# The one-hot of the segment ends in the first layer: one broad VectorE comparison against four narrow ones

## The chip, the cores and the metric

The kernel runs on one core of one Trainium2 chip. The metric is the device time of a run in microseconds (us). The profile is of one execution of its own.

## The reference, cut to what matters

Two graph layers over 6250 nodes with 128 features and 206250 edges (200000 drawn ones, and a loop for each node), sorted by destination. The first layer takes, for each edge, two small matrix products with relu, and then for each destination the maximum over its edges:

```python
e = jnp.concatenate([h_i, h_j - h_i], axis=-1)
m = jax.nn.relu(e @ W2 + b2)
m = jax.nn.relu(m @ W3 + b3)
out = jax.ops.segment_max(m, dst, num_segments=N_NODES)
```

After it come a residual sum and a layer norm, then a second layer (softmax attention over the edges of a destination, a small perceptron, a norm over the nodes) and a last layer norm. The change touches the first layer alone.

## The kernel before

**Tiles and passes.** The edges are cut into 1612 tiles of 128. Four tiles make a group (`GT`), 13 groups a pass (`GROUPS`), and there are 31 passes, so the first layer has 403 groups. Each of the engines PE, ACT, DVE and SP runs a hardware loop over the passes with the 13 groups written out in it; the helper `groups` writes the stages of an engine in a fixed order, each stage some groups behind the newest one.

**GpSimd (POOL).** It writes out all 1612 gathers of the first layer one after the other (L453): each fetches the 128 rows of `q_tab` that a column of `srcT` names, and puts them into `G`. `G` holds a whole pass; a gather of group k waits only for the matmuls of group k - 13 that read its place. After the first layer POOL clears a buffer (L463, L464), and in the second layer it gathers rows of `x1_tab` by the same line.

**SyncE (SP)** loads a window of `p_tab` for each tile (L324) and two broadcast rows of `meta` for half a pass at a time (L332). The second kind waits until DVE has scanned the same half of the pass before.

**TensorE (PE)**, per group: `pre` (L740, L741: gathered rows and window summed in PSUM), `mm3` one group behind (L747), `tr_s` three behind (L753: the scanned maxima are transposed), and `pick` five behind (L762: the transposed maxima times the one-hot `EOH` of the segment ends, so that each segment's last running maximum lands in the column of its node).

**ScalarE (ACT)**, per group: two operations that make the one-hot `OH` (L534, L540), the relu (L545), and the copy out of PSUM after `tr_s` (L550).

**VectorE (DVE)**, per group, in this order: `add_up(0)` six groups behind (L977, adds a tile's picked columns to `accT`), `scan` two behind (L960, a running maximum over 512 edges), `add_up(1)`, `ends` four behind (L966), `add_up(2)`, `add_up(3)`. Each `add_up` waits for the one before it, since their columns may overlap, and reads where to add from a table of destinations (L239). `ends` is the operation that the change replaces: `endT[:, t]` holds for each edge of tile t the number of its node within the window if it is the last of its segment, and -1 otherwise; `EOH` is 1 where the number equals the column number. There are three `EOH` buffers in turn. PE waits in `pick` for the semaphore `eoh_ok`.

The names `Z`, `bank`, `iota_n`, `endT` in rows of the profile: `Z` is the large SBUF tensor that holds `OH`, `EOH`, `S` and other buffers, `bank` is PSUM, the others are SBUF tensors of their own.

Of the kernel before, what the change touches and what calls it, by code (L numbers as in the profile page):

```python
# [12 lines left out]
GT = 4  # L13
# [24 lines left out]
def build(nc, x, src, dst, W1, b1, W2, b2, W3, b3, we_dst, we_src, be, w_proj, b_proj,  # L38
          w1, bb1, w2, bb2, gamma, beta, out):
    fp32, bf16, i32 = mybir.dt.float32, mybir.dt.bfloat16, mybir.dt.int32  # L40
    ALU, ACT = mybir.AluOpType, mybir.ActivationFunctionType
    ds = bass.ds
# [15 lines left out]
    with ctx:  # L58
        def sb(name, shape, dt=fp32):
            return ctx.enter_context(nc.sbuf_tensor(name, shape, dt))  # L60

        def sem(name):
            return ctx.enter_context(nc.semaphore(name))


        ident, iota_n, ones = sb("ident", [128, 128]), sb("iota_n", [128, 128]), sb("ones", [128, 128])
        W1s, W2s, Wpq, W3s = sb("W1s", [128, 128]), sb("W2s", [128, 2, 128]), sb("Wpq", [128, 2, 128]), sb("W3s", [128, 128])
        wprojs, w1s, w2s = sb("wprojs", [128, 128]), sb("w1s", [128, 2, 128]), sb("w2s", [128, 128])
# [6 lines left out]
        srcT, relT, endT = sb("srcT", [128, TILES], i32), sb("relT", [128, TILES]), sb("endT", [128, TILES])  # L75
        rows = sb("rows", [128, TILES])
        cont = rows[0:1, :]
        base = rows[64:65, :].bitcast(i32)
# [13 lines left out]
        def z(shape, dt=fp32):  # L92

            n = 1
            for s in shape:
                n *= s
            words = n if dt != bf16 else n // 2
            assert top[0] + words <= ZW
            part = Z[:, top[0]:top[0] + words]
            top[0] += words  # L100
            assert top[0] <= ZW, top[0]
            if dt != fp32:
                part = part.bitcast(dt)
            if len(shape) == 2:
                part = part.rearrange("p (a b) -> p a b", a=shape[0])
            if len(shape) == 3:
                part = part.rearrange("p (a b c) -> p a b c", a=shape[0], b=shape[1])
            return part
# [19 lines left out]
        EOH = [z([GT, 128]) for _ in range(3)]  # L128
# [34 lines left out]
        consts, pads, prep = sem("consts"), sem("pads"), sem("prep")  # L163
# [7 lines left out]
        dist_ok, oh_ok, x_mm, relu_ok, v_mm, scan_ok, s_tr, st_ok, eoh_ok, o_mm, acc_ok = (sem(n) for n in (  # L171
            "dist_ok", "oh_ok", "x_mm", "relu_ok", "v_mm", "scan_ok", "s_tr", "st_ok", "eoh_ok", "o_mm", "acc_ok"))
# [18 lines left out]
        def after(eng, s, n):  # L191

            if not isinstance(n, int) or n > 0:
                eng.wait_ge(s, n)
# [42 lines left out]
        def bases(engine, t, n):  # L237

            _, got = nc.values_load_multi_w_load_instructions(base[0:1, ds(t, n)], engines=(engine,), min_val=0, max_val=NP - 128,  # L239
                                                             skip_runtime_bounds_check_because="a destination is a node, so below N")  # L240
            return got
# [17 lines left out]
        def used2(k, g):  # L259

            return k if g == 0 else k - 1

        def ring(g):
            return 2 if g == GROUPS - 1 else g % 2
# [147 lines left out]
        def _(pool):  # L412
# [4 lines left out]
            nc.gpsimd.memset(X[:, :, F + 1:TAB], 0.0).then_inc(pads, 1)  # L417
            nc.gpsimd.memset(X[:, :, F:F + 1], 1.0).then_inc(pads, 1)
            nc.gpsimd.iota(iota_n[:, :], pattern=[[1, 128]], base=0, channel_multiplier=0, allow_small_or_imprecise_dtypes=True).then_inc(consts, 1)
            nc.gpsimd.iota(neg_p, pattern=[[0, 1]], base=0, channel_multiplier=-1, allow_small_or_imprecise_dtypes=True).then_inc(consts, 1)  # L420
            nc.gpsimd.memset(ones[:, :], 1.0).then_inc(consts, 1)
            nc.gpsimd.memset(eps[:, :], EPS).then_inc(consts, 1)
# [4 lines left out]
                                    pattern=[[-1, 128]], channel_multiplier=1).then_inc(consts, 1)  # L427
# [27 lines left out]
            for k in range(PASSES * GROUPS):  # L455
                g = k % GROUPS
# [32 lines left out]
        def _(act):  # L489
# [11 lines left out]
                    act.dma_start(to, of.rearrange("(n a) -> n a", a=1)).then_inc(weights_in, 16)  # L501
                act.dma_start(BE, be.rearrange("(n a) -> n a", a=1).broadcast_to([128, 1])).then_inc(weights_in, 16)
            act.wait_ge(weights_in, 16 * 18)
            act.wait_ge(consts, 7)


            def x_evac(h, p, w):
# [180 lines left out]

        @block.tensor
        def _(pe):  # L690
            pe.wait_ge(consts, 7)

            def tr_x(h, p, w):
                pe.wait_ge(x_st[p], h - p + 2)
# [61 lines left out]
            def pick(k, g, i):  # L756

                pe.wait_ge(st_ok, k + 1)
                pe.wait_ge(eoh_ok, k + 1)
                after(pe, acc_ok, used2(k, g) * GT)  # L760
                for j in range(GT):
                    last = nc.tensor.matmul(bank[6 + g % 2][:, j * 128:(j + 1) * 128], STs[ring(g)][:, j * 128:(j + 1) * 128],  # L762
                                            EOH[ring(g)][:, j, :], start=True, stop=True)
                last.then_inc(o_mm, 1)

            groups(pe, [(0, pre), (1, mm3), (3, tr_s), (5, pick)])

            def tr_1(h, p, w):
# [127 lines left out]
        def _(dve):  # L896
            v = nc.vector
# [11 lines left out]
            v.tensor_copy(srcF[R], S0[R]).then_inc(prep, 1)  # L909

            dve.wait_ge(weights_in, 16 * 18)
            dve.wait_ge(consts, 7)
            v.tensor_copy(Wpq[:, 1, :], W2s[:, 1, :])

            v.tensor_tensor(wprojs[0:127, :], wprojs[0:127, :], wproj0[0:127, :], ALU.subtract)
# [47 lines left out]
            def ends(k, g, i):  # L963

                after(dve, o_mm, k - 1)
                v.tensor_tensor(EOH[ring(g)], iota_n[:, :].unsqueeze(1).broadcast_to([128, GT, 128]),  # L966
                                endT[:, ds(k * GT, GT)].unsqueeze(2).broadcast_to([128, GT, 128]), ALU.is_equal).then_inc(eoh_ok, 1)

            def add_up(j):
                def f(k, g, i):  # L970
# [7 lines left out]
                return f  # L978

            groups(dve, [(6, add_up(0)), (2, scan), (6, add_up(1)), (4, ends), (6, add_up(2)), (6, add_up(3))])  # L980


# [201 lines left out]
```

## Time and profile before

| | before |
|---|---|
| median of 3 runs | 4552.47 us (4547.58 to 4559.55) |
| profiled execution, its own time | 4550.18 us |
| its span, from the first to the last instruction | 4548.3 us |
| mean granted TensorE clock | 0.84 |
| POOL busy | 3277.4 us |
| first layer's gathers | 91.4 to 2151.2 us of the span |

Times in the rows are microseconds from the start of the span, or nanoseconds where "mean ns" or "duration ns" is said. A busy engine isn't the bound by that alone; what ended the idle time before an instruction tells more.

### The profile page before, as it was taken

What the parts mean: (1) busy time and instruction counts of PE and PEld (TensorE: products, weight loads), DVE (VectorE), ACT (ScalarE), POOL (GpSimd) and SP (SyncE); (2) the same over time, 40 slices, a digit from 0 to 9 for tenths busy, and PEclk for the clock granted to TensorE, in tenths of its full rate; (3) what the DMA queues carried; (4) which work ended last, traced back from release to release, by engine and by line L of the source; (5) the groups of instructions that cost most, each with busy time, mean ns of one, the idle gap of its engine ahead of it and who ended that gap; (6) DMA issues with size and microseconds to landing.
All of it is one profiled execution on the core that took longest, in us unless ns stands there. A gap on an engine that the chain in (4) does not pass through costs nothing.

```text
span 4548.3 us, 93656 instructions
## 1 busy us (share of the span) xinstructions
PE 3411.8 (75%) x19691; PEld 2455.3 (54%) x19691; DVE 2244.1 (49%) x5106; ACT 2123.6 (47%) x3882; POOL 3277.4 (72%) x3272
## 2 busy tenths in 40 slices
PE   4698888888888888888486666766777667676756
PEld 3587777777677777777244433433444344343432
DVE  2365555555555555555544444444444444444446
ACT  2454444444444444444445444544454454454434
POOL 3777777777777777777477777777777777777740
PEclk9899999999999999999657877787686777767767
DMA  5655555454555545454123223222222222232210
GB/s 124 182 172 164 152 154 158 144 168 144 165 151 152 159 145 166 146 165 116 62 75 81 75 74 79 77 74 74 78 77 75 75 81 75 75 81 74 75 42 28
DMA packets 409331, 503.91 MB, mean 111 GB/s; under 512 B 101159, under 2 KB 330081, under 8 KB 409118
## 3 DMA queue, kind: packets, MB, share of 16 engines
q1 hardware_dynamic: 301598, 284.83, 19.9%
q0 software_dynamic: 104832, 216.49, 19.3%
q14 instruction: 195, 1.60, 0.1%
q10 hardware_dynamic: 2690, 0.73, 0.1%
q8 instruction: 16, 0.26, 0.0%
HBM read 486.41 MB, written 15.26 MB: 110 GB/s over the span
## 4 chain that ended last, share of the span: by engine, by line
POOL 55%; issue 19%; PE 17%; DMA 4%; DVE 2%; SPq 1%; DVEq 1%; ACT 1%; POOLq 0%; ACTq 0%
POOL G L453 55%; PE bank L740 3%; PE bank L741 2%; PE bank L762 2%; PE bank L747 2%; DMA G<-q_tab,srcT 2%; PE bank L841 2%; PE bank L806 1%; PE bank L753 1%; DMA G<-x_tab,srcT 1%; SPq L282 1%; SPq L306 0%; PE bank L709 0%; PE bank L868 0%; DMA cont_d<-Z 0%
## 5 line engine op out<-in xcount | busy, mean ns | idle before, releaser
L453 POOL DMA_INDIRECT G<-x_tab,srcT x1612 | 1658.2, 1029 | 496.0 <-issue 486.5
L453 POOL DMA_INDIRECT G<-q_tab,srcT x1612 | 1568.7, 973 | 510.7 <-issue 484.7
L1091 DVE SCALAR_TENSOR_TENSOR Z<-Z,evr,bank 128x128 f32 x1612 | 560.7, 348 | 741.0 <-PE bank L841 605.3
L841 PE MATMUL bank<-Z 128*128 128x128 f32 x3224 | 860.6, 368 | 51.6 <-DVE Z L1091 50.1
L977 DVE TENSOR_TENSOR accT<-accT,bank 128x128 f32 x1612 | 452.3, 281 | 850.8 <-PE bank L762 620.4
L740 PE MATMUL bank<-ident,G 128*128 128x128 f32 x3224 | 669.3, 291 | 234.2 <-DMA G<-q_tab,srcT 185.6
L628 ACT ACTIVATE Z<-G,evr 128x128 f32<-128x128 f32 x1612 | 597.0, 396 | 424.9 <-PE bank L841 404.2
L841 PEld LDWEIGHTS bank<-Z 128*128 128x128 f32 x3224 | 564.5, 227 | 397.9 <-issue 253.1
L806 PE MATMUL bank<-Z 128*26 128x128 f32 x3224 | 715.8, 319 | 3.7 <-ACT Z L598 3.7
L740 PEld LDWEIGHTS bank<-ident,G 128*128 128x128 f32 x3224 | 519.6, 203 | 258.2 <-issue 257.5
L741 PE MATMUL bank<-Z 128*128 128x128 f32 x3224 | 655.1, 287 | 0.0
L960 DVE TENSOR_TENSOR_SCAN Z<-Z,bank 128x512 f32<-128x512 bf16 x403 | 515.7, 1280 | 79.1 <-PE bank L747 59.7
L741 PEld LDWEIGHTS bank<-Z 128*128 128x128 f32 x3224 | 520.8, 203 | 0.0
L747 PE MATMUL bank<-Z,W3s 128*128 128x512 f32 x806 | 432.5, 619 | 83.0 <-DVE Z L960 83.0
L545 ACT ACTIVATE Z<-bank 128x512 f32<-128x512 f32 x403 | 240.6, 597 | 543.1 <-PE bank L741 512.3
L550 ACT COPY Z<-bank 128x512 f32<-128x512 f32 x403 | 235.8, 585 | 505.2 <-PE bank L762 496.3
L762 PE MATMUL bank<-Z 128*128 128x128 f32 x3224 | 440.9, 281 | 11.7 <-DVE accT L977 11.7
L762 PEld LDWEIGHTS bank<-Z 128*128 128x128 f32 x3224 | 403.2, 197 | 19.6 <-DVE accT L977 15.5
L806 PEld LDWEIGHTS bank<-Z 128*26 128x26 f32 x3224 | 246.4, 114 | 215.8 <-issue 62.8
L753 PEld LDWEIGHTS bank<-ident,Z 128*128 128x128 f32 x1612 | 207.8, 145 | 223.0 <-issue 222.2
L534 ACT ACTIVATE Z<-Z,cols 128x512 bf16<-128x512 bf16 x403 | 291.6, 724 | 42.2 <-DMA Z<-meta 42.2
L813 PE MATMUL bank<-ident,G 128*26 128x128 f32 x124 | 37.7, 404 | 341.7 <-DMA G<-x_tab,srcT 341.7
(152 smaller groups left out, 2613.7 us busy)
## 6 DMA issues: line engine op xcount, KB each, us to landing
Z<-p_tab SPq DMA_DIRECT2D x1612, 64.0 KB
Z<-meta SPq DMA_DIRECT2D x62, 896.0 KB
Z<-meta SPq DMA_DIRECT2D x62, 832.0 KB
Z<-meta SPq DMA_DIRECT2D x62, 768.0 KB
G<-q_tab,srcT POOLq DMA_INDIRECT x1612
G<-x_tab,srcT POOLq DMA_INDIRECT x1612
Z<-ld_d SPq DMA_DIRECT2D x1612, 0.5 KB
x_tab<-X SPq DMA_DIRECT2D x13, 264.0 KB, 2.1
```

The lines of the kernel that those rows point to most:

```text
L453: return pool.indirect_dma_start(to, None, of, bass.IndirectOffsetOnAxis(ap=srcT[:, t:t + 1], axis=0))
L534: nc.scalar.activation(SQ[ring(g)], bc[:, 0, g * CH:(g + 1) * CH], ACT.Square, bias=neg_p).then_inc(dist_ok, 1)
L628: nc.scalar.activation(Gs[u], G[:, s * SC + j, 1:F + 1], ACT.Copy, scale=evr[:, s, 0, j:j + 1]).then_inc(gs_ok, 1)
L740: nc.tensor.matmul(o, G[:, g * GT + j, 0:F], ident[:, :], start=True, stop=False)
L741: last = nc.tensor.matmul(o, Pwin[:, g * GT + j, :], OH[ring(g)][:, j * 128:(j + 1) * 128], start=False, stop=True)
L747: nc.tensor.matmul(bank[2 + g % 2][:, :], W3s[:, :], M1[ring(g)], start=True, stop=True).then_inc(v_mm, 1)
L762: last = nc.tensor.matmul(bank[6 + g % 2][:, j * 128:(j + 1) * 128], STs[ring(g)][:, j * 128:(j + 1) * 128], EOH[ring(g)][:, j, :], start= ...
L806: nc.tensor.matmul(bank[4 + s][0:SC, 0:T], LWd[:, s, j * SC:(j + 1) * SC], OH2[j // HC][:, j % HC * T:(j % HC + 1) * T], start=(j == 0), s ...
L841: nc.tensor.matmul(bank[u][:, 0:128], Gs[u], EQ[j // HC][:, j % HC, :], start=True, stop=True).then_inc(t_mm, 1)
L960: v.tensor_tensor_scan(out=S[ring(g)], data0=bc[:, 1, g * CH:(g + 1) * CH], data1=bank[2 + g % 2][:, :], initial=NEG if first else S[ring( ...
L977: v.tensor_tensor(win, win, bank[6 + g % 2][:, j * 128:(j + 1) * 128], ALU.add).then_inc(acc_ok, 1)
L1091: v.scalar_tensor_tensor(out=win, in0=win, scalar=evr[:, s, 1, j:j + 1], in1=bank[(s * SC + j) % 4][:, 0:128], op0=ALU.mult, op1=ALU.add). ...
```

## The change

A second constant `iota_2` of 128 x 128 x 2 numbers holds every column number twice, and `iota_w` is every second element of it. `ends` becomes four VectorE instructions for a group, one for each tile: `iota_w` compared with one number per partition, column t of `endT`. Each of the four counts up `eoh_ok`, and `pick` waits for four times as many. POOL makes `iota_2` in its setup, so three engines wait for 8 constants in place of 7.

```diff
+        iota_2 = sb("iota_2", [128, 128, 2])
+        iota_w = iota_2[:, :, 0]
...
+            nc.gpsimd.iota(iota_2[:, :, :], pattern=[[1, 128], [0, 2]], base=0, channel_multiplier=0, allow_small_or_imprecise_dtypes=True).then_inc(consts, 1)
...
-            act.wait_ge(consts, 7)
+            act.wait_ge(consts, 8)
...
-                pe.wait_ge(eoh_ok, k + 1)
+                pe.wait_ge(eoh_ok, (k + 1) * GT)
...
                 after(dve, o_mm, k - 1)
-                v.tensor_tensor(EOH[ring(g)], iota_n[:, :].unsqueeze(1).broadcast_to([128, GT, 128]),
-                                endT[:, ds(k * GT, GT)].unsqueeze(2).broadcast_to([128, GT, 128]), ALU.is_equal).then_inc(eoh_ok, 1)
+                for j in range(GT):
+                    v.tensor_scalar(EOH[ring(g)][:, j, :], iota_w, endT[:, ds(k * GT + j, 1)], None, ALU.is_equal).then_inc(eoh_ok, 1)
```

## Rows read from the trace of the kernel before

**Rows 1.** The page: the chain that ended last, shares by engine.

```profile
POOL 55%; issue 19%; PE 17%; DMA 4%; DVE 2%; SPq 1%; DVEq 1%; ACT 1%; POOLq 0%; ACTq 0%
```

**Rows 2.** The page's groups of gathers: busy us, mean ns | idle before.

```profile
L453 POOL DMA_INDIRECT G<-x_tab,srcT x1612 | 1658.2, 1029 | 496.0 <-issue 486.5
L453 POOL DMA_INDIRECT G<-q_tab,srcT x1612 | 1568.7, 973 | 510.7 <-issue 484.7
```

**Rows 3.** All gathers of L453: ns min/median/max, and what ended POOL's idle time.

```profile
L453 POOL DMA_INDIRECT G<-q_tab,srcT x1612: 940/944/2559, 91.4 to 2150.2; - x180
...
  PE bank L741: 6.4, 21
```

**Rows 4.** Waits in the first layer (101 to 2150 us): us in total, times, longest.

```profile
PE bank L740 <- DMA G<-q_tab,srcT: 184.4, 97, 5.1
DVE accT L977 <- issue: 144.8, 40, 8.6
```

**Rows 5.** Timeline, a gather and an L966 that began before it: POOL, then DVE.

```profile
1184.12 1.17 POOL L453 DMA_INDIRECT G<-q_tab,srcT  x1 [0.30 <-issue]
...
1183.79 0.68 DVE L966 TENSOR_TENSOR Z<-iota_n,endT 128x512 f32<-128x512 f32 x1
```

**Rows 6.** Timeline, a gather and an L966 that began after it: POOL, then DVE.

```profile
1006.88 0.94 POOL L453 DMA_INDIRECT G<-q_tab,srcT  x1 [0.31 <-issue]
...
1007.15 0.68 DVE L966 TENSOR_TENSOR Z<-iota_n,endT 128x512 f32<-128x512 f32 x1
```

**Rows 7.** Timeline in the second layer, a gather begun under L1091: POOL, then DVE.

```profile
3104.49 0.94 POOL L453 DMA_INDIRECT G<-x_tab,srcT  x1 [0.31 <-issue]
...
3104.42 0.35 DVE L1091 SCALAR_TENSOR_TENSOR Z<-Z,evr,bank 128x128 f32 x1 [0.40 <-PE bank L841]
```

**Rows 8.** Timeline of the first three gathers of the first layer: DVE, then POOL.

```profile
91.49 1.02 DVE L934 TENSOR_SCALAR Z<-Z 124x1664 bf16<-124x1664 f32 x1
92.42 1.03 DVE L935 TENSOR_SCALAR Z<-Z 124x1664 bf16<-124x1664 f32 x1
...
93.79 1.89 DVE L940 TENSOR_TENSOR Z<-Z 124x1664 f32<-124x1664 int32 x1
95.71 1.03 DVE L941 TENSOR_SCALAR Z<-Z 124x1664 bf16<-124x1664 f32 x1
...
91.39 1.24 POOL L453 DMA_INDIRECT G<-q_tab,srcT  x1 [19.57 <-ACT relT L522]
92.94 1.34 POOL L453 DMA_INDIRECT G<-q_tab,srcT  x1 [0.30 <-issue]
94.58 2.28 POOL L453 DMA_INDIRECT G<-q_tab,srcT  x1 [0.30 <-issue]
```

**Rows 9.** VectorE groups by shape: busy us, mean ns | idle before.

```profile
L966 DVE TENSOR_TENSOR Z<-iota_n,endT 128x512 f32<-128x512 f32 x403 | 276.1, 685 | 0.0
...
L1003 DVE TENSOR_TENSOR mean<-stats 128x52 f32<-128x52 f32 x2 | 0.5, 250 | 0.1
...
L1005 DVE TENSOR_TENSOR tmp<-tmp 128x52 f32<-128x52 f32 x2 | 0.4, 213 | 0.1
...
L913 DVE COPY Wpq<-W2s 128x128 f32<-128x128 f32 x1 | 0.2, 219 | 0.0
...
L937 DVE TENSOR_SCALAR Z<-Z 124x13 f32<-124x13 f32 x1 | 0.2, 173 | 0.0
```

**Rows 10.** Timeline of DVE, one group's step and the start of the next.

```profile
1063.27 0.29 DVE L977 TENSOR_TENSOR accT<-accT,bank 128x128 f32 x1 [1.49 <-PE bank L762]
...
1064.96 0.68 DVE L966 TENSOR_TENSOR Z<-iota_n,endT 128x512 f32<-128x512 f32 x1
1065.56 0.28 DVE L977 TENSOR_TENSOR accT<-accT,bank 128x128 f32 x1
1066.00 0.29 DVE L977 TENSOR_TENSOR accT<-accT,bank 128x128 f32 x1 [0.15 <-DVE accT L977]
1067.25 0.29 DVE L977 TENSOR_TENSOR accT<-accT,bank 128x128 f32 x1 [0.96 <-PE bank L762]
```

More of the change, by code:

```diff
@@ L690, in _ @@
         def _(pe):
-            pe.wait_ge(consts, 7)
+            pe.wait_ge(consts, 8)
             def tr_x(h, p, w):
@@ L911, in _ @@
             dve.wait_ge(weights_in, 16 * 18)
-            dve.wait_ge(consts, 7)
+            dve.wait_ge(consts, 8)
             v.tensor_copy(Wpq[:, 1, :], W2s[:, 1, :])
```

## The prediction

> **What bounds the kernel now.** I read the chain that ended last first [rows 1]: 55% of the span is POOL and 19% is "issue"; PE, the busiest engine by the page, has 17% of the chain. POOL does almost nothing in that time but gathers [rows 2]: 1568.7 us of the first layer's 2060 are inside gathers, and 484.7 are the 0.30 us between two of them that nothing but issue explains. The reader is to see that POOL never rests for anybody: its waits for PE come to 6.4 us in the whole layer [rows 3]. PE, on the contrary, waited 184.4 us for gathered rows [rows 4], some 6 us in each of 31 passes. So the first layer is as long as 1612 gathers with their gaps, and the work of DVE, where the change is made, costs only what it does to the gathers.
>
> Next the spread of one gather [rows 3]: minimum 940, median 944, but mean 973 ns [rows 2]. A few are much longer. The excess is 1612 x (973 - 944) = 46.7 us. The first four gathers take 1.24, 1.34, 2.28 [rows 8] and 2.56 us (the maximum in [rows 3], the fourth in order), which is 3.6 us over four times 0.944, beside setup work that stays as it is. 43.1 us are left. Which instruction do they come from? The timeline shows it. The gather that starts at 1184.12 takes 1.17 us; an L966 had begun at 1183.79 and ended at 1184.47, 0.35 us into the gather [rows 5]. Where an L966 starts after the gather did, the gather takes its 0.94 us [rows 6]. So a gather does something near its start (it reads its column of `srcT`) that can't be done while L966 runs, and it goes on when L966 ends; the extra time is what is left of L966 less 0.12 us (0.35 - 0.12 = 0.23 = 1.17 - 0.94). L966 is the one VectorE operation of this layer that reads two SBUF tensors; L977 and L960 read one and a bank of PSUM. As a check: gathers start every 1.28 us, and a block of h us placed by chance costs (h - 0.12)²/(2 x 1.28) us. For h = 0.685 [rows 9] that is 0.125 us, times 403 is 50 us, near the 43 that are there. The Trainium skill, SBUF — State Buffer, section Who interferes with whom, says the same: a VectorE instruction with two SBUF inputs contends with a GpSimd instruction that reads SBUF. The trace agrees, by the 43 us.
>
> **The change, part by part.**
>
> 1. *L966 goes.* With it goes its hold on the gathers: -43 us, if what replaces it holds nothing. Its own 0.685 us of DVE time don't lie on the path.
>
> 2. *Four comparisons come, one SBUF row and one number per partition each.* What do they hold? Two bounds. The lower one is nothing: L1091 reads an SBUF tensor, a bank and a number per partition out of SBUF, and a gather that starts 0.07 us after it takes 0.94 us [rows 7]. That has the number per partition, and one SBUF tensor, as the new instruction has. The upper bound is in setup [rows 8]: L934, L935 and L941, comparisons with one SBUF tensor, run at two elements a cycle (1664 elements in 1.03 us, against 1.89 for L940 on as many), and they do hold gathers, at two places. The second gather begins at 92.94 under L935 (until 93.45) and is 0.40 us too long, 0.51 - 0.12: the place near its start. And the first ends at 92.63, 0.12 after L934; the third at 96.86, 0.12 after L941: a second place some 0.82 us into a gather, which L966 doesn't touch. So it matters whether the new instruction runs at the double rate. All those that do, and are long enough to be told, read their row in steps of one. The new one reads in steps of two. The one comparison with a stepped source is L937, 13 elements in 173 ns [rows 9]; from the 0.15 to 0.16 us that any operation takes beside its elements, one a cycle gives 0.17 to 0.18 and two a cycle 0.165 to 0.175. It doesn't decide. I take the single rate, hold nothing, -43 us, and price the double rate below.
>
> 3. *How long are they?* At the single rate 128 elements take 0.26 to 0.29 [rows 10]; the number per partition adds up to 0.07 (L1091's 0.35 [rows 7] against L977's 0.28); the steps add up to 128 x (250 - 213)/52 ns = 0.09, from L1003 with stepped sources against L1005 without [rows 9]. So 0.28 to 0.44 each. Two successive operations overlap by about 0.08 (L966 would end at 1065.64, L977 begins at 1065.56 [rows 10]), so four take 0.9 to 1.5 in place of 0.68: +0.2 to +0.8 us a group.
>
> 4. *What hides it.* DVE's step lasts 3.02 us from 1063.27 to 1066.29, then 0.96 idle for PE [rows 10]; the loading of the next destinations, which I estimate at 0.5 of that idle time, comes on top. 3.5 + 0.8 = 4.3 us against 4 x (0.944 + 0.30) = 4.98 that POOL needs for a group. Over a pass of 13 groups 8.8 us are left, and DVE's loop turn takes about 144.8/40 = 3.6 us of issue [rows 4]. DVE fits. It is late by up to 0.8 us for `scan` and `add_up` of the next group, and so is PE where it follows DVE; PE's 184 us of waiting for rows cover that. If the cover were gone, 0.8 x 403 = 322 us would show. SP's broadcast waits for scans; a scan that is 1 us late moves it by 1 us of the pass that it has.
>
> 5. *Small ones.* The larger constant: POOL writes 256 elements more ahead of its list loads, which I put at +0.3 (one element a cycle or two, as VectorE's rows have it). Three more semaphore counts: nothing waits for the first three alone. The register work for three more columns of `endT` is done while the scan before it runs. At the layer's end the last comparisons follow one another with nothing to hide them: +1.
>
> Sum: 4550.2 - 43.1 + 0.3 + 1 = 4508.4 for an execution like the profiled one. The median of the runs is 2.3 us above it, so 4511 us, 0.9% faster. The second layer has 1612 x (1029 - 944) = 137 us of the same delays [rows 2], from another line; where its comparisons fall against the gathers will shift by chance, which I estimate at 10 us either way.
>
> **The rivals.**
>
> *Both ports, at little or even cost.* If the stepped comparison runs at the double rate it holds gathers at both places. With a hold of h, four in each group, the delay is 1612 x (h² + (h - 0.12)²)/(2 x 1.25) us. For h: L913, a copy of 128 elements at the double rate, takes 0.219 [rows 9]; less the overlap 0.14; with the number per partition 0.21; with the steps 0.25. That gives 13, 34 and 51 us, against the 43 that go: 30 faster, 9 faster, 8 slower. So about 4520 at the low end and 4540 to 4560 in the middle, no change that can be told. For it: part 2's own rows; against it: steps of one in all of them. The Trainium skill speaks for this rival: Vector Engine (DVE) Microarchitecture Reference, section Performance modes — why throughput varies by op and dtype, names for the two-port mode one source, both tensors in SBUF and an even outermost extent, and no condition on the step. No row here shows it.
>
> *Both ports, dear.* If successive ones don't overlap, h is 0.33 and the delay 98 us: 55 slower, 4607. If a waiting gather weren't let in between two of the four, they would act as one block of 1.0 us: 403 x (1.0² + 0.88²)/2.5 = 286, 243 slower, 4795. Against the last: the third gather got its first place between L940 and L941, 0.03 us apart [rows 8]. It decides from h = 0.23.
>
> *DVE becomes the bound.* At 0.6 us a comparison its step is 3.5 + 1.5 = 5.0 us, a pass 65 + 3.6 = 68.6 against 66.4 now (13 x 4 x 1.278): 31 x 2.2 = 70 slower, 4620. It decides from about 0.5 us each; the rows give at most 0.44.
>
> *It does nothing:* the gathers are held by something else that comes in the same moment, and stay at 973 ns. 4552. Against it: the sum from L966 alone, 50 us, leaves nothing of the 43 for another cause.
>
> **How the numbers follow.** Forecast (hold nothing) 0.45. Both ports: little cost 0.10, even 0.25, dear 0.11. DVE bound 0.04. Nothing happens 0.05. A measurement of this kernel tells 0.3%, 14 us, from no change. Faster: 0.45 and 0.10, less 0.01 for chance in the second layer, 0.54; same 0.30; slower 0.16. The likeliest case alone spans 4500 to 4523. The range for 8 in 10 reaches over the even case and part of the dear one: 4497 to 4580.
>
> **What the profile after would show.** Right: first layer's gathers with mean near 946 ns, the last of them starting near 2108 in place of 2150, POOL's waits for PE still under 20 us, the new line 1612 times at 0.28 to 0.44 us. Both ports: the new line at 0.22 to 0.33 us, with many gathers of 1.0 to 1.25 us. DVE bound: POOL waits for PE, and PE no longer for rows. The prediction is wrong if the stepped read doesn't keep the instruction to one port.

## The result, and the profile after

The changed kernel takes 4523.35 us (median of 4 runs, 4518.22 to 4528.1) against 4551.94 for the kernel before in the same session (4 runs, 4547.58 to 4559.55). The ratio is 0.9935, with a 95% interval of 0.9921 to 0.995: 28.6 us, 0.65% faster. The profiled execution of the changed kernel took 4528.10 us, the longest of its four; its span is 4526.3 us, its granted clock 0.837.

The page of the changed kernel: the chain's shares, then groups with busy us, mean ns | idle before. L456 is what L453 was, L970 the new comparison, L980 the old L977, L744 the old L741.

```profile
POOL 53%; issue 20%; PE 16%; DVE 4%; DMA 4%; DVEq 2%; SPq 1%; ACT 1%; POOLq 0%; ACTq 0%
...
L456 POOL DMA_INDIRECT G<-x_tab,srcT x1612 | 1664.6, 1033 | 495.9 <-issue 486.4
L456 POOL DMA_INDIRECT G<-q_tab,srcT x1612 | 1531.2, 950 | 509.9 <-issue 483.2
...
L970 DVE TENSOR_SCALAR Z<-iota,endT 128x128 f32<-128x128 f32 x1612 | 361.6, 303 | 0.0
```

The gaps are what they were (483.2 against 484.7 in [rows 2]); the first layer's gathers lost 37.5 us. The instructions of L456 in the changed kernel (ns min/median/max, first and last start in us, and what ended POOL's idle time):

```profile
L456 POOL DMA_INDIRECT G<-q_tab,srcT x1612: 940/944/2558, 93.2 to 2114.5; - x180
L456 POOL DMA_INDIRECT G<-x_tab,srcT x1612: 940/944/2732, 2208.3 to 4362.9; - x180
...
  PE bank L744: 7.9, 26
```

The median gather is the same and POOL still waits for nobody; the excess over the median shrank from 44.7 us to 7.2 (counting the 1608 gathers behind the first four), and the last gather starts at 2114.5 where it started at 2150.2 [rows 3].

The waits of the changed kernel between 101 and 2150 us (us in total, times, longest):

```profile
PE bank L750 <- DVE Z L963: 127.4, 30, 5.4
PE bank L743 <- DMA G<-q_tab,srcT: 103.7, 47, 5.1
```

PE waits 103.7 us for rows in place of 184.4 [rows 4]: faster gathers use up its cover and don't exhaust it.

The two profiled executions, added up in us (before, after, difference):

| | before | after | |
|---|---|---|---|
| first gather starts | 91.4 | 93.2 | +1.8 |
| gathers of the first layer, busy | 1568.7 | 1531.2 | -37.5 |
| last `q_tab` gather starts | 2150.2 | 2114.5 | -35.7 |
| second layer's gathers, busy | 1658.2 | 1664.6 | +6.4 |
| span | 4548.3 | 4526.3 | -22.0 |

Between -35.7 and -22.0 lie some 0.8 us at the first layer's end and 12.7 us in the second layer, whose code is the same: 6.4 of them are gathers, the rest is at its end. The runs of the changed kernel spread over 10 us, and the profiled one is the slowest of them; the medians differ by 28.6. In the +1.8 there is POOL's new constant (POOL's setup: busy us, mean ns):

```profile
L422 POOL IOTA iota<- 128x256 f32 x1 | 1.5, 1513 | 0.0
...
L421 POOL IOTA iota_n<- 128x128 f32 x1 | 0.2, 235 | 0.0
```

It moves the issue of the list load `in_src` from 10.58 to 12.07 us. But the list itself comes 5.4 us later (timeline of VectorE, before, then after):

```profile
33.03 1.03 DVE L909 CAST Z<-Z 124x1664 f32<-124x1664 int32 x1 [32.91 <-DMA Z<-in_src]
...
38.46 1.03 DVE L912 CAST Z<-Z 124x1664 f32<-124x1664 int32 x1 [38.34 <-DMA Z<-in_src]
```

And in the experiments below the first gather starts anywhere from 92.5 to 96.4 us with this same setup, at 92.3 in the kernel before. So how much of the 1.8 is the constant isn't shown.

**Where ports are met.** Four comparisons in the changed kernel, undisturbed (timeline: start us, us):

```profile
1001.75 0.87 DVE L970 TENSOR_SCALAR Z<-iota,endT 128x128 f32<-128x128 f32 x4
```

Each takes 0.28 and the next starts 0.196 after it. Here a gather starts under them:

```profile
1108.51 1.04 POOL L456 DMA_INDIRECT G<-q_tab,srcT  x1 [0.30 <-issue]
...
1108.06 0.87 DVE L970 TENSOR_SCALAR Z<-iota,endT 128x128 f32<-128x128 f32 x4
```

The third of the four runs at 1108.51, from 1108.45 to 1108.73. The gather is 0.10 us too long: 0.22 less 0.12, the rule of [rows 5], for the one comparison that runs and not for the block that lasts until 1108.93. So the gather is let in between two of the four. In all, 131 gathers are more than 10 ns above the median, by 6.3 us together, and none by more than 0.11. That is less than the 0.16 that a comparison of 0.28 us could give, because a comparison that has only just begun doesn't delay a gather: of the 35 gathers that start 0.02 to 0.06 us after a comparison does, 33 keep their 0.94 us. And here the comparisons meet the middle of a gather:

```profile
760.74 0.94 POOL L456 DMA_INDIRECT G<-q_tab,srcT  x1 [0.31 <-issue]
...
761.21 1.02 DVE L970 TENSOR_SCALAR Z<-iota,endT 128x128 f32<-128x128 f32 x4
```

The gather has its 0.94, and the block takes 1.02 in place of 0.87: one of the four was held. The line's durations show how often and how much (its mean is 303, the page says):

```profile
L970 DVE TENSOR_SCALAR Z<-iota,endT x1612: 259/282/515, 164.6 to 2132.8; 128x128 f32<-128x128 f32 x180
```

Those that are held begin 0.48 to 0.75 us into a gather. That is DVE's time, and DVE has time here.

### The profile page after: what moved, and what is told of

It is laid out like the page before. It is cut to its first block, busy times and chain, and to the rows that moved or that the text cites. A ratio compares the mean times of both kernels' runs of the same rounds, so it can differ in the third digit from the quotient of the medians.

```text
span 4526.3 us, 96396 instructions
## 1 busy us (share of the span) xinstructions
PE 3399.4 (75%) x19691; PEld 2442.7 (54%) x19691; DVE 2322.8 (51%) x6315; ACT 2123.9 (47%) x3882; POOL 3247.6 (72%) x3273
## 4 chain that ended last, share of the span: by engine, by line
POOL 53%; issue 20%; PE 16%; DVE 4%; DMA 4%; DVEq 2%; SPq 1%; ACT 1%; POOLq 0%; ACTq 0%
POOL G L456 53%; PE bank L844 2%; PE bank L765 2%; PE bank L743 2%; PE bank L750 2%; PE bank L744 2%; PE bank L809 2%; DMA G<-q_tab,srcT 1%; PE bank L756 1%; DVE accT L980 1%; DVE Z L970 1%; DMA G<-x_tab,srcT 1%; DMA Z<-in_src 1%; SPq L308 0%; PE bank L712 0%
## 5 line engine op out<-in xcount | busy, mean ns | idle before, releaser
L456 POOL DMA_INDIRECT G<-x_tab,srcT x1612 | 1664.6, 1033 | 495.9 <-issue 486.4
L456 POOL DMA_INDIRECT G<-q_tab,srcT x1612 | 1531.2, 950 | 509.9 <-issue 483.2
L1094 DVE SCALAR_TENSOR_TENSOR Z<-Z,evr,bank 128x128 f32 x1612 | 560.8, 348 | 740.9 <-PE bank L844 599.8
L980 DVE TENSOR_TENSOR accT<-accT,bank 128x128 f32 x1612 | 452.2, 281 | 684.5 <-PE bank L765 478.5
L743 PE MATMUL bank<-ident,G 128*128 128x128 f32 x3224 | 648.6, 284 | 148.8 <-DMA G<-q_tab,srcT 103.7
L744 PE MATMUL bank<-Z 128*128 128x128 f32 x3224 | 640.8, 281 | 0.0
L743 PEld LDWEIGHTS bank<-ident,G 128*128 128x128 f32 x3224 | 507.0, 198 | 161.8 <-issue 161.1
L750 PE MATMUL bank<-Z,W3s 128*128 128x512 f32 x806 | 447.7, 639 | 127.4 <-DVE Z L963 127.4
L744 PEld LDWEIGHTS bank<-Z 128*128 128x128 f32 x3224 | 507.0, 198 | 0.0
L970 DVE TENSOR_SCALAR Z<-iota,endT 128x128 f32<-128x128 f32 x1612 | 361.6, 303 | 0.0
```

The lines of the kernel that those rows point to most:

```text
L456: return pool.indirect_dma_start(to, None, of, bass.IndirectOffsetOnAxis(ap=srcT[:, t:t + 1], axis=0))
L743: nc.tensor.matmul(o, G[:, g * GT + j, 0:F], ident[:, :], start=True, stop=False)
L744: last = nc.tensor.matmul(o, Pwin[:, g * GT + j, :], OH[ring(g)][:, j * 128:(j + 1) * 128], start=False, stop=True)
L750: nc.tensor.matmul(bank[2 + g % 2][:, :], W3s[:, :], M1[ring(g)], start=True, stop=True).then_inc(v_mm, 1)
L970: v.tensor_scalar(EOH[ring(g)][:, j, :], iota_w, endT[:, ds(k * GT + j, 1)], None, ALU.is_equal).then_inc(eoh_ok, 1)
L980: v.tensor_tensor(win, win, bank[6 + g % 2][:, j * 128:(j + 1) * 128], ALU.add).then_inc(acc_ok, 1)
```

## The experiments

**What chips they ran on.** The chips that took the experiments run this kernel in about 5900 us, before the change or after it, and every comparison below is with runs of the kernel before on the same chip. The groups of the kernel before there (busy us, mean ns | idle before):

```profile
L453 POOL DMA_INDIRECT G<-x_tab,srcT x1612 | 1605.9, 996 | 1433.3 <-ACT Z L628 973.8
...
L453 POOL DMA_INDIRECT G<-q_tab,srcT x1612 | 1527.7, 948 | 959.8 <-remote 476.8
```

The median gather lasts as long as elsewhere (946 ns), but POOL stands still between them. Its timeline, PE, then ACT, then POOL:

```profile
1048.39 0.39 PE L741 MATMUL bank<-Z 128*128 128x128 f32 x2
...
1051.58 0.60 ACT L545 ACTIVATE Z<-bank 128x512 f32<-128x512 f32 x1 [3.88 <-remote]
...
1049.31 0.95 POOL L453 DMA_INDIRECT G<-q_tab,srcT  x1 [0.30 <-issue]
1051.74 0.95 POOL L453 DMA_INDIRECT G<-q_tab,srcT  x1 [1.48 <-remote]
```

L545 waits for matmuls that end near 1048.8, and begins 2.8 us later. The same place in the changed kernel on its first chip:

```profile
1012.68 0.39 PE L744 MATMUL bank<-Z 128*128 128x128 f32 x2
...
1013.20 0.60 ACT L548 ACTIVATE Z<-bank 128x512 f32<-128x512 f32 x1 [0.67 <-PE bank L744]
```

It begins 0.1 us after the matmuls' end. Over all groups the median of this delay is 2.7 us in the one case and 0.12 in the kernel before on its first chip. PE's word to the others comes late on the experiments' chips, a group takes 6.1 us in place of 5.0 (the mean from scan to scan), and gathers don't bound the first layer. Nor the second one: POOL waits 973.8 us there for ACT's L628, where it waited 4.6 on the first chip, and TensorE's granted clock is 0.52 in that layer (nearly all of it at the lower level, 1.2 GHz) where it was 0.76; in the first layer it is 0.92 against 0.94. So **the total time can't decide there what the change is worth where gathers bind**; what can be read is the length of each gather and of each comparison. The table has both. "Delayed" counts, of 1608 gathers (all but the first four), those more than 10 ns above the run's own median, and "by" is the sum of what they are above it; on the first chip these were 179 and 43.9 us before the change, 131 and 6.3 after it. "First layer" is from the fifth gather's start to the last one's, in the profiled execution.

| run | comparison, for a group | ratio [95%] | gather mean ns | delayed | by, us | median ns of one | first layer, us |
|---|---|---|---|---|---|---|---|
| before_again | one, two tensors, 512 | (one run, 5919.29) | 948 | 8 | 0.6 | 684 | 2458.4 |
| e0_after_again | four, step 2 | 1.0022 [1.0013, 1.0031] | 948 | 22 | 0.8 | 281 | 2469.9 |
| e1_step1 | four, step 1 | 1.0025 [1.0013, 1.0036] | 948 | 12 | 0.4 | 281 | 2462.4 |
| e8_step1 | the same | 1.0028 [1.0017, 1.0039] | 946 | 14 | 0.6 | 281 | 2466.4 |
| e2_narrow_tt | four, two tensors | 1.0024 [1.0013, 1.0035] | 952 | 63 | 6.9 | 285 | 2464.0 |
| e6_narrow_tt | the same | 1.0035 [1.0022, 1.0047] | 952 | 61 | 6.6 | 284 | 2466.9 |
| e9_halves_tt | two, two tensors, 256 | 1.0002 [0.9993, 1.0012] | 953 | 267 | 9.1 | 418 | 2462.4 |
| e4_broad_ts | one, step 2, 512 | (one run, 5908.39) | 953 | 88 | 7.6 | 537 | 2451.4 |
| e3_no_ends | none | 0.9885 [0.9869, 0.9902] | 948 | 1 | 0.1 | - | 2447.9 |
| e7_no_ends | none | 0.9884 [0.9868, 0.9901] | 945 | 2 | 0.1 | - | 2452.7 |
| e5_second_layer | as after, and the second layer's split | 1.0333 [1.0316, 1.035] | 948 | 18 | 0.7 | 281 | 2466.8 |
| e10_second_again | the same | 1.0385 [1.0369, 1.0401] | 946 | 15 | 0.5 | 281 | 2469.8 |

Means that differ by 2 or 3 ns say nothing of delays here: the median itself is 944 to 947 ns from run to run.

**The two kernels again**, with no edit in either.

> The changed kernel once more, on the chip of the following runs. In the runs so far the kernel before takes 5900 us, not 4552, and there PE's semaphore after L744 is raised 2.9 us after that matmul begins (0.29 us in the first profile), so the steps of PE, ACT and DVE last over 6 us and not the gathers bound the first layer. If that holds here too: the freed gathers gain nothing, and the longer DVE step costs 0.2 to 0.9 us in a part of the groups, ratio 1.001 to 1.005. If the kernel before takes 4552 here: ratio 0.992 to 0.995.

> The kernel before with a profile on this chip, as the counterpart of the runs here. Where steps and not gathers bound the first layer: L966 holds gathers as before (single delays up to 0.5 us), but POOL waits for PE in every group, so that the delays vanish in those waits. In the first layer DVE's idle time for PE is longer than 1.2 us in a step.

The 43 us of delays are not there even in the kernel before: 0.6 us are. With the group's rhythm fixed by PE, its L966 misses the gathers' starts. The change costs 13 us there (0.2%).

**The row in steps of one.** All else as in the change:

```diff
-                    v.tensor_scalar(EOH[ring(g)][:, j, :], iota_w, endT[:, ds(k * GT + j, 1)], None, ALU.is_equal).then_inc(eoh_ok, 1)
+                    v.tensor_scalar(EOH[ring(g)][:, j, :], iota_n[:, :], endT[:, ds(k * GT + j, 1)], None, ALU.is_equal).then_inc(eoh_ok, 1)
```

> The four comparisons of the changed kernel, but they read the constant row in steps of one. The changed kernel's comparison takes 282 ns, and up to 515 where it begins 0.48 to 0.75 us into a gather. Theory H (it runs at the double rate and holds both ports whatever the step; what helped is that each of the four is short): 0.22 to 0.28 us each at the median, still up to some 0.5 us in the same place of a gather, gathers of the first layer 948 to 951 ns in the mean, time within 5 us of the changed kernel's 4523 us. Theory S (the step of two keeps the comparison to one port, and that is why the gathers are freed): the step-one comparison holds gathers at two places, their mean goes to 955 to 970 ns, 10 to 30 us slower than the changed kernel.

> The same kernel as e1_step1 (the four comparisons read the constant row in steps of one), once more, in order to have its time where the gathers bound the first layer. If the step does nothing: ratio 0.992 to 0.995, as the changed kernel's 0.9935. If the step of two were what helps: 0.996 to 1.002.

The comparison, first with steps of one and then, on such a chip too, the changed kernel's with steps of two:

```profile
L970 DVE TENSOR_SCALAR Z<-iota_n,endT x1612: 260/281/503, 188.0 to 2626.9; 128x128 f32<-128x128 f32 x180
```

```profile
L970 DVE TENSOR_SCALAR Z<-iota,endT x1612: 259/281/519, 192.1 to 2636.8; 128x128 f32<-128x128 f32 x180
```

The two agree in minimum and median, in the maximum to 16 ns, and the ratios agree: the step does nothing. So both hold one port pair or both hold two; the broad form tells which.

**One broad comparison of the new kind**, with 512 elements. It compares all four tiles with the first one's numbers, so the other three tiles' ends are left out.

```diff
-                for j in range(GT):
-                    v.tensor_scalar(EOH[ring(g)][:, j, :], iota_w, endT[:, ds(k * GT + j, 1)], None, ALU.is_equal).then_inc(eoh_ok, 1)
+                v.tensor_scalar(EOH[ring(g)], iota_w.unsqueeze(1).broadcast_to([128, GT, 128]), endT[:, ds(k * GT, 1)], None, ALU.is_equal).then_inc(eoh_ok, GT)
```

> One comparison of 512 elements with one number per partition (all four tiles are compared with the first tile's ends, so three of four are wrong), the row in steps of two. It tells rate and hold. Double rate: 0.42 to 0.67 us. Single rate: 0.75 to 1.1 us. If it holds both ports (theory H), gathers are held by what is left of it at their start, 403 x (h - 0.12)^2/2.5 us, 15 us for 0.42 and 49 for 0.67, and perhaps at their second place too: mean 955 to 980 ns. If one SBUF row in steps of two holds nothing, the mean is 946 ns whatever the length.

```profile
L969 DVE TENSOR_SCALAR Z<-iota,endT x403: 461/537/710, 192.6 to 2617.5; 128x512 f32<-128x512 f32 x135
```

Undisturbed it takes 0.48 us. At one element a cycle 512 take L966's 0.685 [rows 9] and the number per partition comes on top; so it runs at the double rate. Two meetings with gathers in its timeline, POOL and DVE:

```profile
1360.28 1.20 POOL L456 DMA_INDIRECT G<-q_tab,srcT  x1 [0.30 <-issue]
...
1360.19 0.48 DVE L969 TENSOR_SCALAR Z<-iota,endT 128x512 f32<-128x512 f32 x1
...
220.74 1.00 POOL L456 DMA_INDIRECT G<-q_tab,srcT  x1 [0.30 <-issue]
...
221.15 0.48 DVE L969 TENSOR_SCALAR Z<-iota,endT 128x512 f32<-128x512 f32 x1
```

The first is the place near the start: 1360.67 - 1360.28 - 0.12 = 0.27, and the gather is 0.26 too long. The second begins 0.41 us into a gather and ends at 221.63; the gather ends at 221.74, 0.11 after it and not at 221.69. That is the second place of [rows 8], reached by the stepped comparison when it is long enough. Up to 710 ns of its own are the third meeting: it began later in a gather and was held itself, as more than half of these comparisons are (the median is 537 ns, not 480).

**Four narrow ones with two tensors**, the old kind in the new size:

```diff
-                    v.tensor_scalar(EOH[ring(g)][:, j, :], iota_w, endT[:, ds(k * GT + j, 1)], None, ALU.is_equal).then_inc(eoh_ok, 1)
+                    v.tensor_tensor(EOH[ring(g)][:, j, :], iota_n[:, :], endT[:, ds(k * GT + j, 1)].broadcast_to([128, 128]), ALU.is_equal).then_inc(eoh_ok, 1)
```

> Four operations for a group as in the changed kernel, but each is the old kind: tensor_tensor of the constant row and the tile's column of end numbers, both read from SBUF. Theory H (length of one hold counts: what is left of the operation at the gather's start, less 0.12 us): operations of 0.28 us some 0.2 apart hold gathers no more than the changed kernel's, the mean is 948 to 952 ns, and the time is within 5 us of 4523 us. Since this kind isn't held by a gather's writes, it stays at 0.28 us with no tail to 0.5. Theory O (one SBUF row in place of two is what freed the gathers): two SBUF rows hold as before, mean 965 to 975 ns, time 4545 to 4555 us.

> The same kernel as e2_narrow_tt, four tensor_tensor operations with two SBUF rows, once more, in order to have its time where the gathers bound the first layer. Theory H (length of a hold): within 5 us of the changed kernel, about 0.993 of the kernel before. Theory O (one SBUF row in place of two): 1.000 of it.

```profile
L970 DVE TENSOR_TENSOR Z<-iota_n,endT x1612: 266/285/341, 189.6 to 2630.0; 128x128 f32<-128x128 f32 x180
...
762.75 1.09 POOL L456 DMA_INDIRECT G<-q_tab,srcT  x1 [0.30 <-issue]
...
762.13 0.89 DVE L970 TENSOR_TENSOR Z<-iota_n,endT 128x128 f32<-128x128 f32 x4
```

(One row of the line's durations, two of the timeline.) It is as long as the new kind, 285 against 281 ns, and it delays gathers near their start by the same rule (0.27 - 0.12 = 0.15). But its longest is 341 ns where the new kind's is 515: in the middle of a gather it isn't held. That is one thing that tells the two kinds apart. The other is how soon they hold. The gather above starts 0.02 us after the last of the four comparisons and waits for it all the same. A gather of e1_step1 that starts as soon after the last of its four (at 360.69) doesn't wait:

```profile
360.73 0.95 POOL L456 DMA_INDIRECT G<-q_tab,srcT  x1 [0.30 <-issue]
...
360.11 0.88 DVE L970 TENSOR_SCALAR Z<-iota_n,endT 128x128 f32<-128x128 f32 x4
```

Of the gathers that start 0.02 to 0.06 us into a comparison, 25 of 25 are delayed in e2 and 21 of 22 in e6; of the new kind's, none of 107 in e0, 1 of 111 in e1 and none of 58 in e8. So in a like rhythm the old kind delays gathers by 6.9 and 6.6 us, the new kind by 0.4 to 0.8. The time doesn't part them: e1 and e2 are equal, e6 is within e8's interval.

**Two halves with two tensors.**

```diff
-                for j in range(GT):
-                    v.tensor_scalar(EOH[ring(g)][:, j, :], iota_w, endT[:, ds(k * GT + j, 1)], None, ALU.is_equal).then_inc(eoh_ok, 1)
+                for j in range(0, GT, 2):
+                    v.tensor_tensor(EOH[ring(g)][:, j:j + 2, :], iota_n[:, :].unsqueeze(1).broadcast_to([128, 2, 128]),
+                                    endT[:, ds(k * GT + j, 2)].unsqueeze(2).broadcast_to([128, 2, 128]), ALU.is_equal).then_inc(eoh_ok, 2)
```

> Two operations of the old kind for a group, 256 elements each, two SBUF inputs. Between one of 512 (43 us of held gathers) and four of 128 (7 to 10). Length of a hold: (0.42 - 0.12)^2/2.5 us for each, 806 of them, 29 us, if they fall on the gathers by chance; in a fixed rhythm with them anything from 10 to 40. Longest single delay (a gather's length less 0.944): about 0.42 - 0.12 = 0.3 us, against 0.51 under the long operation and 0.15 under the short. By number of SBUF inputs alone all three would be alike.

```profile
883.46 1.20 POOL L456 DMA_INDIRECT G<-q_tab,srcT  x1 [0.30 <-issue]
...
883.42 0.75 DVE L970 TENSOR_TENSOR Z<-iota_n,endT 128x256 f32<-128x256 f32 x2
```

The first half runs from 883.42 to 883.84, 0.38 us beyond the gather's start, and the gather is 0.26 too long. Had the pair held as one block, until 884.17, it would have been 0.59. Its ratio is no change, the least of the split forms' cost.

**No comparison at all.** The one-hot is filled once ahead of the layer, and DVE's comparison in each group is left out, so that the maxima are picked at wrong columns:

```diff
-            groups(dve, [(6, add_up(0)), (2, scan), (6, add_up(1)), (4, ends), (6, add_up(2)), (6, add_up(3))])
+            groups(dve, [(6, add_up(0)), (2, scan), (6, add_up(1)), (6, add_up(2)), (6, add_up(3))])
...
-                pe.wait_ge(eoh_ok, (k + 1) * GT)
+                pe.wait_ge(eoh_ok, 9)
```

> No comparison in the loop: the three buffers are filled once ahead of the first layer with the ends of the first tiles and never again, so the maxima are picked at wrong columns. It is the floor: what is left of the delays, and what the four comparisons cost DVE. If the 6 us of delays that are left in the changed kernel come of the comparisons: mean 946 ns (the first four gathers alone), layer's gathers 6 us shorter than the changed kernel's, 4512 to 4520 us. If another operation holds gathers too, the mean stays at 949 to 950.

> The same kernel as e3_no_ends (no comparison in the loop, the picked maxima are wrong), once more, in order to have its time where the gathers bound the first layer. The whole of what the comparisons cost: first layer's gathers at 946 ns, 43 us less than the kernel before in the gathers, ratio 0.990 to 0.992. A ratio below 0.985 would say that DVE's own time lies on the path too.

Both are 1.15% faster, 68 to 70 us, and that isn't the price of the comparisons. The gathers of e7, and of the kernel before on such a chip (first and last start):

```profile
L456 POOL DMA_INDIRECT G<-q_tab,srcT x1612: 938/944/2558, 92.6 to 2553.9; - x180
L456 POOL DMA_INDIRECT G<-x_tab,srcT x1612: 938/944/2186, 2688.8 to 5651.0; - x180
```

```profile
L453 POOL DMA_INDIRECT G<-q_tab,srcT x1612: 939/946/2556, 92.3 to 2559.3; - x180
L453 POOL DMA_INDIRECT G<-x_tab,srcT x1612: 939/946/2396, 2698.5 to 5731.8; - x180
```

The first layer's gathers end 5 us earlier, the second layer's take 2962 us from first to last in place of 3033, in code that is the same. They are shorter themselves, 974 to 977 ns in the mean where every run with a comparison and the same second layer has 996 or 997, which is some 35 of the 71 us. Why the second layer went faster wasn't tried. In the first layer the old comparison costs 6 to 11 us on these chips (2458.4 less 2452.7 and 2447.9), and no more can be taken from these runs.

**The second layer's comparisons split in the same way.** The second layer's broad comparison, 1664 elements of two tensors, becomes 13 narrow ones:

```diff
-                v.tensor_tensor(EQ[c], iota_n[:, :].unsqueeze(1).broadcast_to([128, HC, 128]),
-                                relT[:, ds(q * SC + c * HC, HC)].unsqueeze(2).broadcast_to([128, HC, 128]), ALU.is_equal).then_inc(eq_ok, 1)
+                for j in range(HC):
+                    part = v.tensor_scalar(EQ[c][:, j, :], iota_w, relT[:, ds(q * SC + c * HC + j, 1)], None, ALU.is_equal)
+                part.then_inc(eq_ok, 1)
```

> The changed kernel, and in the second layer the one-hot of 13 tiles (one operation of 1664 elements, 1.89 us, two SBUF inputs) is made tile by tile in the same way: 13 comparisons of 0.28 us. The second layer's gathers lose some 140 us to the long operation. If length of one hold counts: 1612 x (0.2 - 0.12)^2/2.5 us is left, their mean falls from 1033 to 946 to 955 ns, and the time falls by 100 to 135 us against the changed kernel, where the second layer is bound by its gathers. Against it: DVE does 13 x 0.2 = 2.6 us in place of 1.9, 124 times, and its sequencer works out 13 addresses, so if DVE or PE takes the bound over, the gain is smaller, 30 to 80 us, and POOL waits.

> The same kernel as e5_second_layer (the one-hot of the second layer tile by tile as well), once more. If the gathers bound the second layer here (kernel before at 4552 us): 100 to 135 us faster than the changed kernel. If the steps do, as in the runs so far: ratio 1.033 again, since 13 comparisons and their addresses stand ahead of PE's sums 124 times.

The page of e5, and its waits between 2720 and 5900 us:

```profile
L456 POOL DMA_INDIRECT G<-x_tab,srcT x1612 | 1528.9, 948 | 1681.5 <-ACT Z L631 1222.0
```

```profile
POOL G L456 <- ACT Z L631: 1222.0, 120, 31.3
...
PE bank L844 <- DVE Z L1086: 345.0, 58, 7.1
```

The gathers are free: 948 ns on average against 996, the longest 1127. And the kernel is 3.3 to 3.9% slower. The 13 comparisons and the register work for their addresses stand in DVE's list ahead of the sums; PE waits 345 us for them, ACT for PE, and POOL for ACT 1222 us in place of 973.8. In e8_step1, on the same chip and with the same first layer, PE waits 476.1 us for the sums (L1094) and here 320.9 (L1095), so that its waits grow by 190 us in all; e5 is 177 us slower than e8. On these chips nothing covers the price of the split. It says nothing of a chip on which gathers bind the second layer, as they do in the first profile (137 us of delays, and 4.6 us of waiting for ACT): there the split wasn't run.

## Why the prediction was right, and where it wasn't

The range, 4497 to 4580, holds the 4523.35, and faster was the likeliest. In part that is luck: the 4511 rests on part 2, which failed, and it is only 12 us off because comparisons as short as these cost little even though they do hold gathers. By its steps:

- **What bounds the kernel, and the 43 us.** Right. The first layer's excess fell by 37.5 us, its end by 35.7, and POOL's waits for PE are 7.9 us.
- **Part 2, "I take the single rate, hold nothing".** This step failed. The stepped comparison runs at the double rate (512 elements in 0.48 us) and meets gathers as the double-rate operations of [rows 8] do: it delays them near the start, at the second place when long, and is held in the middle of one. L1091 [rows 7] was a wrong neighbour: it reads PSUM beside SBUF, and of the 206 gathers of the second layer that start with more than 0.15 us of it left, none is over 0.02 us too long; L934 and L941 [rows 8] were the right ones. The step of two, by which the prediction set them apart, does nothing (281 ns either way).
- **The rival that came true is "both ports, at little cost"**, which gave about 4520 and had 0.10. The Trainium skill, Vector Engine (DVE) Microarchitecture Reference, section Performance modes — why throughput varies by op and dtype, names no condition on the step for the two-port mode; the 480 ns of the broad form agree.
- **Its price formula had the wrong second term.** For a hold of 0.21 it gave 34 us: 1612 x 0.09²/2.5 = 5.2 us near the start and 1612 x 0.21²/2.5 = 28.4 at the second place. Measured are 6.3 in all, and none at the second place that can be found. A comparison of 0.28 us that begins before 0.48 us in a gather is over by 0.76, before the gather comes to its second place at 0.82; one that begins later is held itself. Only a two-port operation longer than 0.82 - 0.48 = 0.34 us can delay a gather there, and the new one isn't. So the even case (0.25) was never open at this length, and its mechanism should have gone to the low end.
- **So the gain comes mainly from shortness**, not from the ports left alone: a gather waits for what remains of the operation that runs, and at most 0.16 us of 0.28 can delay it where 0.565 of 0.685 could. This is shown by the longest delay in each form: 0.51 us for 685 ns with two tensors, 0.26 for 418, 0.15 for 285; at the double rate 0.25 for 480 and 0.11 for 282. The new kind adds something of its own, since it holds only from some 0.07 us after its start and the old one from 0.02. What the old kind, cut in four, would gain where gathers bind wasn't run. An estimate by the prediction's own formula, with delays of up to 0.14 us: 1612 x 0.14²/2.5 = 12.6 us of delays would be left against the 6.3 measured, so that some 31 us would be gained in place of 37.
- **Part 3.** Right: 0.28 us each, and successive ones overlap by 0.086.
- **Part 4.** Right: DVE's busy time rose from 2244.1 to 2322.8 us and PE's waits for rows, 103.7 us of them left, covered it. On the experiments' chips it isn't covered in full: the first layer grows with DVE's time per group, from 2447.9 and 2452.7 without a comparison and 2451.4 with 0.54 us to 2458.4 with 0.68 and 2462 to 2470 with 0.75 to 0.89. That order is a reading of single executions, which differ by some 5 us between like kernels.
- **Part 5.** The constant takes POOL 1.5 us in place of 0.3 (1513 ns for 128x256 elements in two dimensions, and 235 for half as many in one), and the first gather starts 1.8 us later; that the one makes the other isn't shown. The layer's end costs 0.8 where 1 was said.
- **The second layer** moved by 12.7 us in the profiled execution, beyond the 10 that were allowed to chance.

In sum, against the 4508.4 us of the prediction: +1.5 for the later first gather, -0.2 at the first layer's end, +5.6 because the gathers lost 37.5 us and not 43.1, and +12.7 in the second layer give 4528.0, and the profiled execution took 4528.10. The terms are read from the same two traces, so that they add up is no test of their causes.

Open are why PE's semaphores come late on some chips, why the second layer moved by 12.7 us, what made it faster in e3 and e7, and whether its split pays where gathers bind.

## What to carry to other kernels

Where GpSimd's gathers bound a stage, look at their mean against their median, and at which VectorE operation lies over the start of the long ones; what counts then is how long each such operation is, and cutting it into short ones took 37 of the 43 us here. Before you cut, see that VectorE has the time: the same cut in the second layer freed its gathers and cost over 3% on chips where gathers didn't bind that layer, because the sums stood behind it in the queue. A total time is worth nothing for such a question on a chip where another engine sets the rhythm; read the durations of the instructions there.

## What the runs showed of the hardware

- A gather of 0.944 us meets VectorE at two places. Near its start it waits for the end of a running operation with two SBUF inputs or at the double rate (what is left, less 0.12 us). A narrow operation with two inputs does this from 0.02 us after its own start, one at the double rate only from some 0.07 us (21 of 22 and 25 of 25 gathers delayed at 0.02 to 0.06 us, against 1 of 276). Later, operations at the double rate alone meet it: begun 0.48 to 0.75 us into the gather they are held (up to 515 ns for 282), and one that still runs at 0.82 us delays the gather to 0.12 us after its end. The Trainium skill, SBUF — State Buffer, section Who interferes with whom, has it that two SBUF inputs contend with GpSimd's reads and not with its writes, and that the two-port mode contends with GpSimd for the shared pair, which is a read port and a write port; a read place and a write place fit what the rows show. It also has whoever comes first keep the ports for the whole instruction, which holds here for VectorE's instructions (the 0.27 us above) but not for the gather: comparisons that begin in its first 0.48 us run undisturbed.
- A waiting gather is let in between two VectorE operations that overlap by 0.086 us.
- The same program takes 4552 us on one chip and 5901 to 5922 on three others. There a matmul's signal reaches ScalarE 2.7 us after its end in the median of the first layer's groups, in place of 0.12, and TensorE's granted clock in the second layer is 0.52 in place of 0.76.
